# Attention step: where the output projection, the third maxima and the sixth masked key copy stand

## What is computed

```
def _L0_xattn_ref(xq, xk, xv, Wq, bq, Wk, bk, Wv, bv, Wo):
    ...
    scores = jnp.einsum('bhnd,bhmd->bhnm', q, k) * scale
    weights = jax.nn.softmax(scores, axis=-1)
    out = jnp.einsum('bhnm,bhmd->bhnd', weights, v)
    out = out.transpose(0, 2, 1, 3).reshape(B, N, EMBED)
    return out @ Wo.T
```

## Time and profile before

| | us |
|---|---|
| median of three runs (511.29 to 514.03) | 511.59 |
| the profiled execution's own time | 511.59 |
| its span, first to last instruction | 509.8 |
| PE busy | 462.5 (91%) |
| DVE busy | 414.7 (81%) |
| ACT busy | 375.2 (74%) |
| POOL busy | 289.6 (57%) |

### The profile page before, as it was taken

One profiled execution on the slowest core, in us unless ns is written; L12 is line 12 of the kernel. 1 busy time (PEld: TensorE's weight loads), 2 busy tenths in 40 slices (PEclk: granted clock), 3 DMA queues, 4 the chain that ended last, 5 costly groups with the idle time before them and its releaser, 6 DMA issues.

```text
span 509.8 us, 21711 instructions
## 1 busy us (share of the span) xinstructions
PE 462.5 (91%) x8732; PEld 317.0 (62%) x8732; DVE 414.7 (81%) x1117; ACT 375.2 (74%) x563; POOL 289.6 (57%) x380
## 2 busy tenths in 40 slices
PE   3999998998889999999996879999999997979996
PEld 1777776664456666666664545656555555768885
DVE  4688667989688988988978788989888865859996
ACT  3888867887887887887887468888888759535550
POOL 4444224685857687786838547799999831012000
PEclk9999999999999999999999899999999999989999
DMA  5376549530011011111111012232332324456664
GB/s 195 83 182 182 145 127 247 164 105 1 3 26 46 27 35 37 26 37 36 27 47 46 3 41 87 71 123 89 107 104 93 127 77 140 138 156 189 187 184 126
DMA packets 53313, 49.25 MB, mean 97 GB/s; under 512 B 14192, under 2 KB 40944, under 8 KB 53232
## 3 DMA queue, kind: packets, MB, share of 16 engines
q1 hardware_dynamic: 53232, 48.13, 31.9%
HBM read 30.81 MB, written 17.04 MB: 94 GB/s over the span
## 4 chain that ended last, share of the span: by engine, by line
PE 34%; DVE 17%; POOL 14%; issue 6%; ACT 3%; DMA 1%; DVEq 0%; SPq 0%; POOLq 0%; ACTq 0%
DVE c_mx L635 10%; PE ps L1558 7%; PE ps L1636 6%; PE ps L863 3%; POOL v_or_front L1045 3%; PE ps L1461 3%; PE ps L965 3%; PE ps L1194 2%; PE ps L834 2%; DVE copies_or_layer L626 2%; POOL e_inv_root L1074 2%; PE ps L896 2%; POOL e_scaled L1356 2%; POOL e_inv_root L1059 2%; POOL k_or_hidden L1364 2%
## 5 line engine op out<-in xcount | busy, mean ns | idle before, releaser
L635 DVE TENSOR_REDUCE c_mx<-ps 128x16 f32<-128x1024 f32 x64 | 78.0, 1219 | 18.9 <-PE ps L834 18.9
L572 POOL TENSOR_TENSOR copies_or_layer<-k_or_hidden,w_mask 128x512 bf16<-128x512 f32 x80 | 83.6, 1071 | 2.6 <-DVE c_work L666 2.6
L737 ACT ACTIVATE c_work<-ps 128x2048 f32<-128x2048 f32 x32 | 59.9, 1872 | 23.2 <-PE ps L863 23.0
L1530 ACT ACTIVATE copies_or_layer<-k_or_hidden 32x512 f32 (+1 forms) x64 | 40.2, 628 | 30.6 <-PE ps L1558 30.0
L1356 POOL TENSOR_TENSOR e_scaled<-e_raw,e_rden 128x512 f32<-128x512 f32 x16 | 20.8, 1300 | 51.1 <-DMA e_rden<-dispatch_inverses 51.1
L1543 DVE TENSOR_TENSOR o_slot_out<-ps,w_b 128x512 f32<-128x512 f32 x64 | 41.2, 686 | 8.6 <-PE ps L1558 8.2
L1407 ACT ACTIVATE e_slot_in<-ps 128x1024 f32<-128x1024 f32 x30 | 30.7, 1023 | 17.2 <-PE ps L1461 17.2
L747 ACT ACTIVATE c_q_bd<-x_all,w_mask 128x512 f32<-128x512 f32 x64 | 42.7, 718 | 0.0
L1636 PE MATMUL ps<-o_slot_out,ctx_sb 128*64 128x129 f32 x512 | 38.0, 286 | 3.3 <-issue 2.7
L1558 PE MATMUL ps<-w_w,copies_or_layer 64*32 64x128 f32 x2048 | 38.6, 277 | 1.6 <-issue 1.6
L592 POOL COPY c_v_bd<-v_or_front 64x512 f32<-64x512 f32 x32 | 21.7, 679 | 30.9 <-PE ps L883 29.7
(11 more groups left out here) (164 smaller groups left out, 1172.9 us busy)
## 6 DMA issues: line engine op xcount, KB each, us to landing
x_all<-x_scratch SPq DMA_DIRECT2D x64, 128.0 KB, 3.1
combine_scratch<-v_or_front SPq DMA_DIRECT2D x16, 512.0 KB, 2.7
ctx_sb<-combine_scratch SPq DMA_DIRECT2D x16, 512.0 KB, 3.3
x_sb<-in_x SPq DMA_DIRECT2D x16, 256.0 KB, 3.2
x_scratch<-a_x SPq DMA_DIRECT2D x16, 256.0 KB, 2.4
ctx_sb<-in_ctx SPq DMA_DIRECT2D x16, 256.0 KB, 3.6
e_rden<-dispatch_inverses SPq DMA_DIRECT2D x64, 64.0 KB, 2.1
out<-o_y SPq DMA_DIRECT2D x32, 128.0 KB, 3.0
```

The costliest lines, as they stand in the source:

```text
L572: ins = nc.gpsimd.tensor_tensor(k_bd[:, c.m2, s, :], k32[:, c.v, :], w["mask8"][:, s:s + 1].to_broadcast([P, TOK]), ALU.mult)
L635: nc.vector.reduce_max(mx[:, c.m2, :, p], ps[:, SCORE:SCORE + 2, :].rearrange("p a (h m) -> p (a h) m", m=N), AX_X).then_inc(mx_sb.sem, 1)
L737: nc.scalar.activation(prob[:, h, :], ps[:, 0:4, :].rearrange("p a b -> p (a b)"), ACT.Exp, scale=float(HD) ** -0.5).then_inc(p_sb.sem, 1)
L1530: ins = self.nc.scalar.activation(self.h_bd[at, c.m2, :, :, e % 2, :].rearrange("p s g k -> p g s k"), self.hidden[at, :, bass.ts(c.v, SC ...
```

## The change

PE: the output projection moves from the end of a step (there for chunk t-1) to the next step, behind the first part of the scores; parts 2 and 3 of the scores move ahead of `turn(t-1, 1)` and of the turning back. DVE: maxima part 0 and key slot 0 move ahead of the addition to x; maxima part 2 moves ahead of the second division; key slot 2 is left out. POOL: makes key slots 2 to 7. ACT: the four query copies are made one at a time, before and between the exponentials. SP: one transfer of the maxima in place of four.

```
-    max_in = kit.landings("c_max_in", 4)
+    max_in = kit.landings("c_max_in")
...
-                for T in range(4):
-                    sp.dma_start(neg_row[32 * T:32 * T + 1, c.m2, :], negmax[16 * T:16 * (T + 1), c.m2, :]).then_inc(max_in.of(c), 16)
+                sp.dma_start(neg_row[0:P:32, c.m2, :], negmax[:, c.m2, :]).then_inc(max_in.of(c), 16)
...
             elif t.k >= 0:
-                masks_k(t.plus(EARLY), range(MASKS_DVE, MASK_SLOTS))
+                masks_k(t.plus(EARLY), range(MASKS_DVE - 1, MASK_SLOTS))
...
             normalise(t.plus(-1), 0)
+            spread_k(t.plus(EARLY), 0)
+            row_max(t.plus(2), 0)
             c = t.plus(-2)
             if c:
                 dve.wait_ge(wo_ps.sem, wo_ps.at(c))
...
-            spread_k(t.plus(EARLY), 0)
-            row_max(t.plus(2), 0)
             spread_k(t.plus(EARLY), 1)
             row_max(t.plus(2), 1)
-            spread_k(t.plus(EARLY), 2)
+            row_max(t.plus(2), 2)
             normalise(t.plus(-1), 1)
...
-            row_max(t.plus(2), 2)
             row_max(t.plus(2), 3)
...
-            if t.k == CHUNKS - 2: spread_q(end, 0)
+            if t.k >= 0: spread_q(t.plus(1), 0, 1)
             exp(t.plus(0), 0)
+            if t.k >= 0: spread_q(t.plus(1), 1, 1)
...
-            if t.k == CHUNKS - 2: spread_q(end, 2)
-            elif t.k >= 0: spread_q(t.plus(1), 0)
+            if t.k >= 0: spread_q(t.plus(1), 2, 1 if t.k < CHUNKS - 2 else 2)
             exp(t.plus(0), 1)
             raw(t.plus(0), 0)
+            if 0 <= t.k < CHUNKS - 2: spread_q(t.plus(1), 3, 1)
...
-            if 0 <= t.k < CHUNKS - 2: spread_q(t.plus(1), 2)
...
             if t.k >= 0: scores(t.plus(2), 0)
+            c = t.plus(-2)
+            if c:
+                pe.wait_ge(oT_sb.sem, oT_sb.at(c))
+                for p in range(PC):
+                    ins = nc.tensor.matmul(ps[:, MISC, p * P:(p + 1) * P], oT[:, p * P:(p + 1) * P], w["woT"][:],
+                                           start=True, stop=True)
+                ins.then_inc(wo_ps.sem, 1)
             values(t.plus(-1), 1)
...
             scores_T(t.plus(0), 1)
+            if t.k >= 0: scores(t.plus(2), 2)
             turn(t.plus(-1), 1)
-            if t.k >= 0: scores(t.plus(2), 2)
             values(t.plus(0), 0)
...
+            if t.k >= 0: scores(t.plus(2), 3)
+            if t.k == CHUNKS - 2: scores_T(end, 0)
             c = t.plus(-1)
             if c:
                 pe.wait_ge(o_norm.sem, o_norm.at(c))
                 for p in range(PC):
                     ins = nc.tensor.transpose(ps[:, MISC, p * P:(p + 1) * P], o_tok[:, c.m2, p, :], w["ident"][:])
                 ins.then_inc(oT_ps.sem, 1)
...
             turn(t.plus(0), 0)
-            c = t.plus(-1)
-            if c:
-                pe.wait_ge(oT_sb.sem, oT_sb.at(c))
...
```

More of the change, by code:

```diff
@@ L561, in masks_k @@
                 return
-            if not slots or slots[0] == MASKS_DVE:
+            if not slots or slots[0] <= MASKS_DVE:
                 if c.plus(-2): pool.wait_ge(sc_ps.sem, sc_ps.at(c.plus(-2)))
-            if not slots or c.v and slots[0] == MASKS_DVE:
+            if not slots or c.v and slots[0] <= MASKS_DVE:
                 pool.wait_ge(q_sb.sem, q_sb.at(c))
@@ L570, in masks_k @@
             for s in slots:
-                if s == MASKS_DVE: pool.wait_ge(k_sb.sem, k_sb.at(c))
+                if s == slots[0] <= MASKS_DVE: pool.wait_ge(k_sb.sem, k_sb.at(c))
                 ins = nc.gpsimd.tensor_tensor(k_bd[:, c.m2, s, :], k32[:, c.v, :], w["mask8"][:, s:s + 1].to_broadcast([P, TOK]), ALU.mult)
@@ L626, in spread_k @@
             ins = nc.vector.tensor_scalar(k_bd[:, c.m2, s, :], k32[:, c.v, :], w["mask8"][:, s:s + 1], None, ALU.mult)
-            if s == 2:
+            if s == MASKS_DVE - 2:
                 ins.then_inc(k_bd_lead.sem, 1)
@@ L953, in _ @@
                 ins.then_inc(oT_ps.sem, 1)
-            if t.k >= 0: scores(t.plus(2), 3)
-            if t.k == CHUNKS - 2: scores_T(end, 0)
             if t.k == CHUNKS - 1:
@@ L960, in _ @@
             turn(t.plus(0), 0)
[L961 to L967, removed]
             if t.k == CHUNKS - 1: dispatch.logits(pe, Chunk(None, 0))
```

## The result

The changed kernel takes 539.55 us (median of six runs, 538.98 to 540.78), against 511.05 us for the kernel before: 1.0568 times as long, interval 1.0538 to 1.0599. I had forecast slower, 529.3 us, with a range up to 534.5. The sign and the place were right, the size was not: +28.5 us where I had +17.7, and the measured time lies 5 us above the range.

A forecast was written before the change was run, and what follows sets the result against it. The prediction saw DVE's maxima and PE bounding the 9.28 us step, with POOL's loop hidden by 0.3 us. Closing that loop gave +16.5, the end +0.5 and +0.65: +17.7 on 511.6, 529.3 us, range 524.5 to 534.5.

The forecast's parts named there:

- the loop through POOL: Scores part 0, values, v_bd copies, q_lead, masked keys, part 0 again: 9.02 us, hidden below the 9.28 us step.
- the two edits that lengthen it: In POOL's loop: the sixth mask on POOL adds 1.00 us, the output projection ahead of the values 0.89.
- The cover of 0.3 us: POOL's last masked key copy ends 0.31 us before part 0 of the next step's scores starts on PE.
- the sum of 10.91 us for the loop, times 11: Steps 2 to 13: POOL's loop 9.02 + 1.00 + 0.89; 120.0 us in place of 103.48, so +16.5.
- My bounds: Main case 526 to 533 us: POOL-to-PE hand-over +1.1, projection at 1.06 +1.9, undisturbed POOL -1.9, end terms varying.
- if the cover of POOL's loop went, these edits would be worth between 0 and 0.35 a step: Single transfer, ACT's order and addition behind the first maxima: between 0 and 0.35 us a step without POOL's longer loop.
- no change: Rival, 4%: POOL's loop stays covered and the step stays 9.28 us; 512.7 us.
- faster: Rival, 3%: PE never waits again, steps 1 to 13 take 8.93 us each, 4.6 us less; 507 us.
- The end: Steps 13 to 16: second division ahead of the fourth maxima +0.5 us, step 16's later projection and addition +0.65.
- The rival that DVE's masks hold POOL off: Two DVE masks each cost POOL their whole 0.48 us, step 0.62 longer, 6.8 us in all; 536 us, 6%.

The follow-up runs named there:

- e5: Kernel before with one edit: key slot 2 goes from DVE to POOL, six masks there; 519.76 us (1.0184).
- e4: Changed kernel with two idle matmuls on PE ahead of part 0 of the scores in steps 1 to 13; 534.25 us (1.0474 against before).
- e8: Changed kernel with the projection back in its old place and five masks on POOL, all other edits kept; 527.44 us (1.0337).
- e10: Kernel before with one edit: key slot 0 and part 0 of the maxima ahead of the addition to x; 519.36 us (1.0197).
- e11: Kernel before with the third maxima ahead of the second division, and parts 2 and 3 of the scores earlier on PE; 519.26 us (1.0174).
- e12: Kernel before with single query copies, the fourth ahead of ACT's copy c_oT, and one transfer of the maxima in place of four; 514.44 us (1.0073).
- e1: Changed kernel with key slot 2 back on DVE, so five masks on POOL; 522.07 us (1.0245 against before).
- e2: Changed kernel with the output projection moved behind the values of the second half, six masks still on POOL; 525.63 us (1.0295 against before).
- e6: Kernel before with the projection behind the next step's part 0 of the scores, and part 0 of the maxima ahead of the addition to x; 521.15 us (1.0210).
- e3: Changed kernel with key slot 2 back on DVE and the projection behind the values, other edits kept; 526.51 us (1.0304 against before).
- e9: Kernel of e3 with the maxima turned behind the transposed scores' second half, and ACT's negation behind its third query copy; 526.39 us (1.0313 against before).

## Why the prediction missed

Right: the loop through POOL, its place, and the two edits that lengthen it. PE waited 1.3 to 2.3 us at part 0 of the scores, ended by L571, where I had 1.5 to 2. The cover of 0.3 us was smaller than I read it: of the 0.31 between POOL's end and part 0, 0.25 is the hand-over from POOL to PE, so only some 0.06 was free. e5 agrees: its masks take 0.81 more than the 5.21 before, and its step is 0.75 longer.

**The step that failed is the sum of 10.91 us for the loop, times 11.** I had 120.0 us for steps 2 to 13; they took 129.8.

- *6.3 us are the clock*, which has no term in my sum. 129.81 - 11 x 11.22 = 6.4; the five steps with a granted clock of 0.86 or 0.87 hold 6.25 of it. A sixth long step, 11.51, has the clock at 1.00: a mask of DVE begins there 0.06 us ahead of POOL's v_bd copies, which take 1.64 in place of 1.35. The last step is 0.17 shorter. I had forecast PE idle of up to 2 us in every step and priced PE's work behind it at full clock all the same. e4 fills the wait and takes 5.7 us of these steps back. As the trace shows, the clock can fall behind such a wait, and fall again in a later turn of the loop; the Trainium skill (TensorE: Matmul & The Clock Gate, HAM oscillation — how this bites in real kernels) describes the same for a loop that waits for a transfer in each turn. There it falls in every turn, here in five of eleven.
- *3.4 us are three small terms*, 0.31 a step. The projection takes 1.09 where the scores precede it, not 0.89 as in the row where a turn precedes it (+0.20). POOL to PE is 0.25, not the 0.05 of DVE to PE (+0.20). The v_bd copies are 0.09 shorter without a DVE mask beside them. My bounds had named the first two, and had 1.9 and 1.1 us for them; each came to 2.2. With these three alone the sum would have been 532.7 us, inside the range. The clock took the time out of it.

**The sentence "if the cover of POOL's loop went, these edits would be worth between 0 and 0.35 a step" was wrong**, and with it the price of two rivals: "no change" at 512.7 and "faster" at 507. e8 has that cover gone and a step of 10.67. I had compared DVE's sums and the loop that was there, and not followed the order of waits: the addition behind part 0 of the maxima (e10: 0.86 a step), the division behind the third maxima (e11: 0.77), the fourth copy ahead of c_oT (e12: 0.44). It did not hurt the forecast, because a step is as long as its longest loop: parts that alone cost 0.75 (the sixth mask), 0.86, 0.77 and 0.44, and the projection with them, cost 1.94 a step together, at full clock.

**The end**: I had +1.15 for steps 13 to 16, and the span from step 13 on was 0.8 shorter. The clock fell there in both executions at different places, so these terms can't be checked.

**The rival that DVE's masks hold POOL off** did not come in the changed kernel at its price of 0.62 a step. The six masks took 6.21, as summed, though here the 0.17 falls on the last mask (1.22) and not on the first. The largest loss of one meeting there is 0.29, in the step of 11.51 (starts 0.06 apart); in e1 it is 0.25 (starts 0.08 apart). By the Trainium skill (SBUF — State Buffer, Who interferes with whom) the later of the two waits for the whole instruction of the other, where DVE is in a two-port mode. POOL would then have lost about 0.4 us in each of these two meetings (0.48 less the 0.06 and 0.08 between the starts); the rows bear out a part of it. For DVE they agree: its mask that begins at 226.16, just behind one of POOL's at 226.14, ends 0.3 us behind the end of POOL's and takes 1.30 in place of 0.48.

Open: which of two equal loops bounds e2 and e6; why the stretch behind step 13 is 4 to 5 us longer in e2, e3 and e9 (its clock is at most a part of it); how much of the 1.39 us in e8 falls to each of its two waits. A version with the projection in the next step and the addition behind the second maxima was not tried.

## What to carry to other kernels

An engine that is busy three quarters of a step can still have no slack: find what starts its work and what waits for its end, and sum that loop before putting anything into it. Count the hand-over from one engine to the next as part of the loop, or the cover looks larger than it is. When a forecast makes PE wait in each turn of a loop, give the work behind the wait a second price at the lower clock: here it cost 0.7 to 1.9 us in each of five turns of eleven, and nothing in e1, where PE waited 1.19 us. And an edit called free under a longer loop should be priced with that loop taken away, wait by wait in the order of the instructions, or undoing the known loss brings back only a part (e3: 13 of 28 us).

## What I had not expected of the hardware

The clock fell in some turns and not in others at the same wait: after 2.01 us the values took 1.09, after 2.00 us 1.91 in the next step. And giving PE two matmuls a step that nobody uses made the whole kernel about 5 us faster. Nor had I expected the hand-over from POOL to PE to take 0.25 us, five times that from DVE to PE.
